# Half-block steps for two halves of the tokens, in the tail of a two-layer decoder kernel

## The reference, cut to what matters

```python
x = x + _L0_xattn_ref(_layernorm(x), ctx_2048, ...)   # softmax attention, 16 heads of 128
x = x + _L0_ffn_ref(_layernorm(x), ...)               # 8 experts of 176 units, top 2, plus 352 shared units
x = x + _L1_xattn_ref(_layernorm(x), ctx_2048, ...)   # linear attention, 16 heads of 16, relu features of 64
x = x + _L1_ffn_ref(_layernorm(x), ...)               # 8 experts of 176 units, top 2, normalised, plus 704 shared
```

```python
scores = jax.nn.softmax(x @ gate_w, axis=-1)
topk_w, topk_idx = jax.lax.top_k(scores, K)
comb = comb.at[jnp.arange(T)[:, None], topk_idx].add(topk_w)
g = silu(einsum('td,edh->teh', x, w_gate)) * einsum('td,edh->teh', x, w_up)
routed = einsum('teh,ehd,te->td', g, w_down, comb)
shared = silu(x @ sw_gate) * (x @ sw_up) @ sw_down
```

## Time and profile before

| | us |
|---|---|
| median of 3 runs | 1308.1 |
| lowest and highest | 1306.59 and 1308.49 |
| the profiled execution | 1307.69 |
| its span, first to last instruction | 1306.0 |
| around the span | 1.7 |

### The profile page before, as it was taken

How to read it: one execution, slowest core, us unless ns; L and a number is a source line. 1 busy time by engine, 2 the same in 40 slices (tenths; PEclk the granted TensorE clock), 3 DMA queues, 4 the chain that set the end, 5 groups by cost and what they waited for, 6 DMA issues and landing times. The chain is left out here.

```text
span 1306.0 us, 27038 instructions
## 1 busy us (share of the span) xinstructions
PE 1199.6 (92%) x9589; PEld 1044.7 (80%) x9589; DVE 884.8 (68%) x1829; ACT 732.5 (56%) x1285; POOL 538.6 (41%) x559
## 2 busy tenths in 40 slices
PE   5999999999879999999999999999999876997798
PEld 4888888889758888888788887888878776785586
DVE  5666656566657887878887788778886465555554
ACT  4656556556545666576665666666656433442443
POOL 2423232232225363553545535445364063562242
PEclk9999999999988999999999999999999967997799
DMA  4211111110031111011110111101000070022000
GB/s 144 69 42 56 39 34 53 39 39 1 2 90 53 48 48 48 1 47 47 47 47 0 47 47 34 60 0 47 0 1 1 1 246 20 2 115 86 1 1 15
DMA packets 38795, 56.04 MB, mean 43 GB/s; under 512 B 3106, under 2 KB 37202, under 8 KB 38226
## 3 DMA queue, kind: packets, MB, share of 16 engines
q1 hardware_dynamic: 37922, 54.23, 13.1%
q10 hardware_dynamic: 816, 1.05, 0.3%
HBM read 54.81 MB, written 0.46 MB: 42 GB/s over the span
## 5 line engine op out<-in xcount | busy, mean ns | idle before, releaser
L1118 POOL TENSOR_TENSOR att_sq<-att_work,att_sq 128x500 fp32r<-128x500 f32 x90 | 119.8, 1331 | 159.7 <-DVE att_sq L1018 159.7
L1122 POOL TENSOR_TENSOR attention_kk<-att_work,attention_kk 128x500 fp32r<-128x500 f32 x90 | 122.1, 1357 | 153.3 <-DVE attention_kk L1026 153.3
L102 PE MATMUL att_csum<-att_pT,att_cn 125*128 125x448 f32 x384 | 156.3, 407 | 5.1 <-DVE att_pT L1067 4.4
L944 ACT ACTIVATE att_pr<-att_pr,att_nmx 112x1500 f32<-112x1500 f32 (+1 forms) x96 | 108.5, 1130 | 72.4 <-DVE att_nmx L1055 72.4
L104 PE MATMUL att_csum<-att_pT,att_cn 125*128 125x448 f32 x384 | 141.1, 367 | 0.0
L103 PE MATMUL att_csum<-att_pT,att_cn 125*128 125x448 f32 x384 | 140.0, 365 | 0.0
L535 DVE SCALAR_TENSOR_TENSOR attention_kk<-kvs_keys_ps,kvs_bk,attention_kk 64x500 fp32r<-64x500 f32 x96 | 70.8, 738 | 91.7 <-ACT attention_kk L419 90.1
L1067 DVE TENSOR_TENSOR att_pT<-att_ring,att_pT 125x448 fp32r<-125x448 f32 x192 | 118.3, 617 | 21.7 <-ACT att_pT L960 21.5
L1052 DVE TENSOR_SCALAR_CACHE_REDUCE att_pr<-att_ring 112x500 f32<-112x500 f32 x192 | 121.8, 675 | 6.4 <-PE att_ring L104 5.0
L290 PE MATMUL kvs_feat<-kvs_f,attention_kk 128*125 128x256 f32 x768 | 113.0, 284 | 10.9 <-DVE kvs_kp L607 10.1
L877 PEld LDWEIGHTS att_ring<-all_ident,att_pr 112*125 112x125 f32 x768 | 110.9, 190 | 14.4 <-ACT att_pr L944 2.2
(11 more groups left out here) (279 smaller groups left out, 3276.9 us busy)
## 6 DMA issues: line engine op xcount, KB each, us to landing
attention_raw_t<-in_ctxT SPq DMA_DIRECT2D x45, 500.0 KB, 4.0
att_raw_n<-in_ctx SPq DMA_DIRECT2D x16, 750.0 KB
tail_gate_w<-in_gate SPq DMA_DIRECT2D x1, 2112.0 KB, 8.1
tail_up_w<-in_up SPq DMA_DIRECT2D x1, 2112.0 KB, 13.9
kvs_raw_q<-in_wq SPq DMA_DIRECT2D x8, 256.0 KB, 4.0
tail_wo_raw<-in_wo SPq DMA_DIRECT2D x4, 512.0 KB, 6.9
tail_down_w<-in_down SPq DMA_DIRECT2D x1, 2048.0 KB, 18.0
tail_gate_w<-in_gate SPq DMA_DIRECT2D x1, 1760.0 KB, 12.0
```

The costliest lines, as they stand in the source:

```text
L102: nc.tensor.matmul(out, w_lo, x_hi, start=start, stop=False, skip_group_check=True)
L944: nc.scalar.activation(pr[:, j, keys], pr[:, j, keys], ACT.Exp, scale=-1.0, bias=nmx[:, j:j + 1], accum_out=z[:, 4 * u + j, c:c + 1]).then ...
L1118: nc.gpsimd.tensor_tensor(sq[1][:, i % 2, :], work[:, i % 2, :], sq[0][:, i % 2, :].bitcast(F32), ALU.subtract).then_inc(sq_lo, 1)
L1122: nc.gpsimd.tensor_tensor(kk[:, c, 2 + gi, :], work[:, i % 2, :], kk[:, c, gi, :].bitcast(F32), ALU.subtract).then_inc(k_lo, 1)
```

## The change

`TT` = 4 tiles become two halves of 224 tokens (`H` = 2, `HT` = 224; tiles 0 and 1, tiles 2 and 3). The two mixtures are no longer two loops of 14 and 17 blocks over 448 tokens but one row of 62 half-blocks, `STEPS`: the 14 blocks of the first mixture for half 0, the same for half 1, the 17 blocks of the second for half 0, then for half 1. A loop over positions 0 to 64 runs on every engine. A step k is widened at position k (from step 28 on, k+1), spread at the same position save for a table of late ones, and narrowed two positions after its spread. Between these steps stand the other works of the other half: the norm and routing of half 1 during steps 0 to 12, the second norm, read-out and third norm of half 0 from position 15 to 28, during half 1's blocks of the first mixture, and those of half 1 from position 29 to 42, during half 0's blocks of the second mixture.

Core of the tables:

```diff
+STEPS = [(m, h, n) for m in range(2) for h in range(H) for n in range(BLOCKS[m])]
+WEIGHTED = (E * EU // 128, BLOCKS[1])
+FIRST1 = H * BLOCKS[0]
+SPLITS = [(0, n) for n in range(BLOCKS[0])] + [(1, n) for n in range(BLOCKS[0], BLOCKS[1])] + \
+         [(1, n) for n in range(BLOCKS[0])]
...
+FULLS, HIDS = 7, 4
...
+    return k if k < FIRST1 else k + 1
...
+def spread_at(k):
+    late = {0: 1, FIRST1: 33, FIRST1 + 1: 33, FIRST1 + 2: 34, FIRST1 + 3: 34, FIRST1 + 4: 35, FIRST1 + 5: 35,
+            FIRST1 + 6: 36, FIRST1 + 7: 36, FIRST1 + BLOCKS[1]: 47}
+    return late.get(k, widen_at(k))
```

```diff
+        dve.wait_ge(self.newton, 11 * h + 1)
+        nc.vector.tensor_scalar(self.rstd[:, y].bitcast(I32), self.var[:, y].bitcast(I32), -0.5, RSQRT_BITS,
+                                ALU.mult, ALU.add).then_inc(self.newton, 1)
...
+        dve.wait_ge(self.newton, n + 1)
+        nc.vector.scalar_tensor_tensor(self.tmp[:, y], self.tmp[:, y], -0.5, self.var[:, y], ALU.mult, ALU.mult)\
+            .then_inc(self.newton, 1)
+        dve.wait_ge(self.newton, n + 2)
+        nc.vector.scalar_tensor_tensor(self.rstd[:, y], self.tmp[:, y], 1.5, self.rstd[:, y], ALU.add, ALU.mult)\
```

On the tensor engine (the old order is removed whole; at r = 5 to 9 stand `features`, `read` and `turn` of the read-out):

```diff
+                    if t == 2 and i == 3:
+                        pe.wait_ge(wo.scaled, 2 * B)
+                        ln1.turn(pe, 0)
+                    if t == 3 and i == 1:
+                        router.logits(pe, 0, ln1)
+            for n in range(POSITIONS):
+                r, h = (n - 15) % 14, (n - 15) // 14
+                if n == 28:
+                    ln3.turn(pe, 0)
+                for k in steps_at(widen_at, n):
+                    moe.widen(pe, k)
+                if n == 1:
+                    router.turn(pe, 0)
+                for k in steps_at(spread_at, n):
+                    moe.spread(pe, k)
+                if n == 6:
+                    router.logits(pe, 1, ln1)
+                if n == 12:
+                    router.turn(pe, 1)
+                if h in (0, 1):
+                    if r == 4:
+                        lin.query(pe, h)
+                    if r == 5:
...
+                    if r == 10:
+                        lin.project(pe, h)
+                if n in (32, 46):
+                    router.turn(pe, 2 + (n - 32) // 14)
+                for k in range(len(STEPS)):
+                    if spread_at(k) + 2 == n:
+                        moe.narrow(pe, k)
+                if n == 4:
+                    ln1.turn(pe, 1)
+                if n in (18, 32):
+                    ln2.turn(pe, (n - 18) // 14)
+                if n == 42:
+                    ln3.turn(pe, 1)
+                if n in (28, 42):
+                    router.logits(pe, 2 + (n - 28) // 14, ln3)
```

On the scalar engine:

```diff
+            ln1.high(act, 0)
+            ln1.copy(act, 0)
+            moe.split_high(act, 3)
+            router.exponentials(act, 0)
+            act.wait_ge(wo.out_done, TT)
+            for n in range(POSITIONS):
...
+                for k in steps_at(widen_at, n):
+                    moe.silus(act, k)
...
+                for k in range(len(STEPS)):
+                    if spread_at(k) + 1 == n:
+                        moe.high(act, k)
+                if n in (12, 32, 46):
+                    router.high(act, {12: 1, 32: 2, 46: 3}[n])
+                if n < 10:
+                    moe.split_high(act, n + 4)
...
+                if n == 5:
+                    ln1.high(act, 1)
+                    ln1.copy(act, 1)
+                if n == 8:
+                    router.exponentials(act, 1)
...
+                if n in (28, 42):
+                    ln3.high(act, (n - 28) // 14)
+                    ln3.copy(act, (n - 28) // 14)
+                if n in (29, 43):
+                    router.exponentials(act, 2 + (n - 29) // 14)
+                if 20 <= n < 34:
+                    moe.split_high(act, n - 20 + 17)
```

On the vector engine, the first half's norm and routing stand ahead of the loop and all the rest in it; read-out and third norm are at the same positions as on PE (`h`, `r`):

```diff
+            wo.add(dve, 0, x_loaded)
+            ln1.statistics(dve, 0, wo.added, 1)
+            ln1.guess(dve, 0)
+            for i in range(3):
+                ln1.sharpen(dve, 0, i)
+            ln1.apply(dve, 0)
+            ln1.low(dve, 0)
+            router.start(dve, 0)
+            router.shares(dve, 0)
+            router.ranks(dve, 0)
+            router.weights(dve, 0)
+            for n in range(POSITIONS):
...
+                for k in steps_at(widen_at, n):
+                    moe.hidden(dve, k)
...
+                if n == 0:
+                    wo.add(dve, 1, x_loaded)
+                    ln1.statistics(dve, 1, wo.added, 2)
+                if n == 2:
+                    ln1.guess(dve, 1)
+                    ln1.sharpen(dve, 1, 0)
+                if n == 3:
+                    ln1.sharpen(dve, 1, 1)
+                    ln1.sharpen(dve, 1, 2)
+                    ln1.apply(dve, 1)
+                if n == 5:
+                    ln1.low(dve, 1)
+                if n == 7:
+                    router.start(dve, 1)
+                if n == 9:
...
+                    moe.add(dve, (n - 15) // 14)
+                if n in (16, 30):
+                    ln2.statistics(dve, (n - 16) // 14, moe.added, (n - 16) // 14 + 1)
+                    ln2.guess(dve, (n - 16) // 14)
+                    ln2.sharpen(dve, (n - 16) // 14, 0)
+                if n in (17, 31):
+                    ln2.sharpen(dve, (n - 17) // 14, 1)
+                    ln2.sharpen(dve, (n - 17) // 14, 2)
+                    ln2.apply(dve, (n - 17) // 14)
...
+                    if r == 11:
+                        ln3.statistics(dve, h, lin.added, h + 1)
+                        ln3.guess(dve, h)
+                        ln3.sharpen(dve, h, 0)
+                    if r == 12:
+                        ln3.sharpen(dve, h, 1)
+                        ln3.sharpen(dve, h, 2)
+                        ln3.apply(dve, h)
+                if n in (28, 42):
+                    ln3.low(dve, (n - 28) // 14)
+                if n in (29, 43):
+                    router.start(dve, 2 + (n - 29) // 14)
+                if n in (30, 44):
+                    router.shares(dve, 2 + (n - 30) // 14)
+                    router.ranks(dve, 2 + (n - 30) // 14)
+                if n in (31, 45):
+                    router.weights(dve, 2 + (n - 31) // 14)
+                if n in (48, POSITIONS - 1):
+                    moe.add(dve, 2 + (n > 48))
```

On POOL:

```diff
+            wo.low(pool, nc.gpsimd, 5)
+            moe.split_low(pool, 0)
+            wo.low(pool, nc.gpsimd, 7)
+            pool.wait_ge(wo.odd_lo, 4)
             pool.wait_ge(halves_set, 2)
-            moe0.set_member(pool, 0)
-            wo.low(pool, nc.gpsimd, 5)
-            pool.wait_ge(wo.odd_lo, 3)
-            moe0.set_member(pool, 1)
-            pool.wait_ge(moe0.member_done, 2)
...
-            moe1.set_member(pool, 0)
-            pool.wait_ge(moe1.member_done, 1)
-            moe1.set_member(pool, 1)
...
+            moe.set_member(pool, 0)
+            pool.wait_ge(moe.member_done, 1)
+            moe.set_member(pool, 1)
+            pool.wait_ge(moe.member_done, 2)
+            for i in range(1, len(SPLITS)):
+                moe.split_low(pool, i)
...
+                if i in (16, 28):
+                    lin.add_bias(pool, (i - 16) // 12)
```

1144 lines of the change are left out of this document (576 added, 568 removed).

## The result

The changed kernel takes 1321.59 us (median of 4 runs, 1320.04 to 1323.23) against 1307.34 us (4 runs, 1305.69 to 1308.49) of the kernel before in the same comparison. The ratio is 1.0108, with a 95% interval of 1.0095 to 1.0122: it is 1.1% slower. The profiled execution took 1321.45 us with a span of 1319.8; forecast were 1323.3 and 1321.6, and the range was 1303 to 1336. The total fits, so what is to be tested is whether its parts do, and why the overlap earned so little.

A forecast was written before the change was run, and what follows sets the result against it. PE bounds the mixtures' regular stretches and waits in the other stages. 1098.7 start + 154.9 half-steps + 24.5 small work + 38.5 waits + 5.0 behind the last matmul = 1321.6 span, + 1.7 = 1323.3 us; 8-in-10 range 1303 to 1336.

The forecast's parts named there:

- first half-block starts at: First mixture's start: first widening at 1098.7 us, not 1107.4; 1093 if no DVE operation meets POOL, 1103 if all small ones do.
- 62 half-steps: Both mixtures on PE: 56 weighted and 6 unweighted half-blocks take 154.9 us, whole ones 136.3; halving costs 18.6 us.
- steps 0 to 5: First mixture's start: PE waits for half 0's weights and half 1's norm turn, with slowed clock, together 10.2 us.
- steps 6 to 27: Rest of the first mixture, with half 0's read-out and second norm on half-loaded DVE and ACT: 2.5 us of waits.
- positions 28 to 33: Change of mixtures: third norm's turn, then DVE's 15 us row against 7 us of PE cover; waits and half clock 20.8 us.
- positions 40 to 47, and rest: Second mixture: 3 us of waits at half 1's third norm and routing, 2 us in the rest of the row.
- small PE work: Between half-blocks: norm turns, logits, weight turns, query, reads and projections keep their price, 24.5 us, within 22 to 31.
- the rival with cheap halves: Mixtures on PE: halves cost nothing, by the skill's formula, with the forecast's waits: 1311 us; chance 0.04.
- The wait of 4.6 us ahead of the turn of half 1: Position 4: PE waits 4.6 us as half 1's norm on DVE stands behind products, low halves and POOL collisions.
- the cover works: Whole tail: start at 1093, half 1's norm and routing in time, PE waits only 18.5 us: 1297.6 us; chance 0.16.
- POOL paces the splits: 14 steps at the start: POOL splits and DVE collisions exceed 2.5 us a position, PE waits 0.7 each: 1333 us; chance 0.12.
- the order serialises elsewhere: An unforeseen engine wait stops the row; overlap is lost in each half's read-out, 17 us idle returns: 1335 us; chance 0.06.

The follow-up runs named there:

- number 11: The kernel before, each whole block issued on PE as two half-blocks in turn (widen, spread, narrow): 1326.87 us against 1307.74, ratio 1.0137.
- number 2: The changed kernel with the first half of set_member ahead of batch 5's low half, the second behind the third split: 1320.8 us against 1307.56, ratio 1.0095.
- number 3: The changed kernel with matmuls that nobody reads put into four of PE's waits: 1322.59 us against 1307.56 of the kernel before, ratio 1.012.
- number 4: The changed kernel with the third routing on DVE ahead of most of half 1's second norm: 1317.35 us against 1307.56 of the kernel before, ratio 1.0075.
- number 7: The changed kernel with one Newton step per norm in place of three: 1315.2 us against 1308.42 of the kernel before, ratio 1.0049.
- number 10: The changed kernel without POOL's low halves of the second mixture's blocks 0 to 13, small memsets instead: 1317.75 us against 1307.74, ratio 1.007.
- number 6: The changed kernel with both routing exponentials computed by the silu function, so no table loads there: 1318.57 us against 1308.42, ratio 1.0064.
- number 5: The kernel before with matmuls that nobody reads in PE's waits at the norms and first spreads: 1302.89 us against 1308.42, ratio 0.995.
- number 9: The kernel before with nearly all PE waits filled, also ahead of the first projection and the logits: 1293.45 us against 1307.74, ratio 0.9909.
- number 12: The changed kernel with set_member early, third routing first, two Newton steps and PE's waits filled: 1310.88 us against 1308.87 of the kernel before, ratio 1.0016.
- number 8: The changed kernel with set_member early, third routing first and two Newton steps per norm: 1314.59 us against 1308.42 of the kernel before, ratio 1.0041.

## Why the prediction was right

**The sum by its terms.** Forecast and measured, in us:

| term | forecast | measured |
|---|---|---|
| first half-block starts at | 1098.7 | 1102.0 |
| 62 half-steps | 154.9 | 56 x 2.525 + 6 x 1.96 = 153.2 |
| waits and half clock, steps 0 to 5 | 10.2 | 3.3 + 5.1 = 8.4 |
| steps 6 to 27 | 2.5 | 1.7 |
| positions 28 to 33 | 20.8 | 5.4 + 1.8 + 8.9 + 6.8 = 22.9 |
| positions 40 to 47, and rest | 5.0 | 2.6 + 3.2 + 1.0 = 6.8 |
| small PE work | 24.5 | what is left: 19.9 |
| behind the last matmul | 5.0 | 4.9 |
| span | 1321.6 | 1319.8 |

The first summands of each wait are gaps, the last one is half the length of PE's work at clock 0.50 behind them (1107.6 to 1117.8, 1192.9 to 1203.1, 1216.7 to 1220.2, 1257.7 to 1264.6). The 19.9 of small PE work is the remainder and takes up the errors of the other terms. Added up in the trace from start to start of PE's matmuls behind 1102.0, the parts are half-steps 150.5, small work 22.9, gaps over 0.75 us 24.6 and, for half of the other time at clock 0.50, 14.9. The table's steps and its gaps both hold the matmul ahead of a gap, and some spreads stand side by side and are cheaper; that is where its remainder lost 3 us.

That the total came within 2 us is in part luck: the start was 3.3 us later than forecast, waits and half clock 1.0 more, the half-steps 4.4 less and the small work 1.6 less.

**The halving.** Right, and shown three times: 2.52 to 2.53 us a step in the changed kernel, the same in number 11, and 19.1 us for the whole against 18.6. The 0.112 us of the earlier trace rows hold in the mixtures: a widening of 224 columns starts every 0.111 us. The Trainium skill (TensorE: Matmul & The Clock Gate, Back-to-back issue gap) would have 96 ns by its formula for a single matmul, and the same section has about 81 ns at 128 and 131 ns at 512 columns for a stream with weight loads. The trace agrees with neither: 111 ns at 224 and 205 at 448 columns, so the rival with cheap halves had no ground.

**The start.** The mechanism was right and was priced too low: the two-column operations did end with POOL's, but four of them and both scalings did, so the turn of half 0 was 9.2 us late and the first widening 3.3 us later than forecast. How much of it is `set_member` stays open: in number 2, with one half of it moved away, 7.6 of the 9.4 us stay, as POOL's splits take that half's place and the other half meets the scalings. The Trainium skill (SBUF — State Buffer, SBUF: two separate sides) calls the port of DVE and GpSimd an exclusive lock, taken by a DVE operation in a two-port mode against any GpSimd one and by one with two inputs in SBUF against a GpSimd operation that reads SBUF. The trace agrees: the one-input L1193 is held 1.88 us by a memset and the two-input L1202 1.79 us by a select, while the two-input operations from 1089.38 on take 0.16 us beside a memset, whose row names no input. So moving POOL work helps only as far as what then stands beside the chain does not hold it.

**Steps 0 to 5.** The wait for the first spread was 3.3 us as forecast. The wait of 4.6 us ahead of the turn of half 1 did not come: PE ran at clock 0.50 from 1107.6 to 1117.8 and was itself late by as much. Number 3 shows the two to be one: with the clock kept up, the wait is 4.2 us and the turn stands at the same place. The prediction added 1.2 us of clock to each wait; it should have seen that a slow PE and a wait for DVE take the same time, not two times. Behind the turn this no longer holds: in number 3 half clock there cost 3.5 us.

**The change of mixtures.** Right in place and order, and nearly in size: 5.4 us ahead of `ln3.turn(0)` (5 forecast, with its clock in it), 1.8 and 8.9 ahead of the weight turn (2.6 and 8). The clock made 6.8 us; the prediction had it inside the first 5 and as 5 us at half clock behind the weights, which it took whole, though such a stretch costs half its length. Numbers 4, 7 and 10 each take a part away, DVE's order 4.9 us of the wait, Newton steps 1.2, POOL's splits 2.2. The table loads are in that chain, as predicted, but with about 1 us (number 6) and not with 2.6.

**Where the overlap's gain went.** Against number 11, which has the halves' price but no overlap, the changed kernel is only 5 us faster. PE's gaps over 0.75 us in the tail sum to 42.8 us, and to 44.8 before. The work that was to hide the norms and routings is there, but a half's routing on DVE is nearly as long as a whole one's: the first takes 4.1 us for two tiles (1099.3 to 1103.4) and took 4.5 for four. Its operations are small and their number sets the time. The same chain is run twice and its cover, four widenings and a narrow, is half as long. POOL's splits come on top where they stand beside such a chain, as at the third norm of half 0 and the second of half 1; the second norm of half 0 (from 1153.7) meets none and keeps its 0.16 us an operation. This paragraph is argued from the traces; no run changes the length of the cover alone.

**The rivals.** That the cover works fell: the start came at 1102 and not 1093. That POOL paces the splits fell: in 1127 to 1188 PE is busy 59.3 of 61 us beside POOL's splits. That the order serialises elsewhere fell too, behind the first widening every gap over 0.75 us is at a place that the prediction names or at most 1.7 us long. The 1335 of that last rival is not the sum of what it names: 1323.3 + 17 would be 1340.

**What stays open.** How the 15.4 us that the filled kernel gains divide between the clock and other effects of the fillers isn't settled; no run held the clock up without matmuls. The two groups of runs in numbers 5 and 9 speak for the clock: with the same fillers, runs at a lower clock were 10.5 and 8.8 us longer. Why the same program keeps its clock in one run and not in another isn't known, and no profile shows one of the longer runs. Nor is it shown what the changed kernel would take with all of `set_member` out of the norm's way.

## What to carry to other kernels

Before an overlap in halves, price a half step from rows with the short moving operand and count each change of stationary operand twice; set against it not the idle time of the bounding engine but the number of small operations in the chain that must fit behind the cover. Where one engine's idle time is followed by its own work on the path, first try to fill the wait with matmuls that nobody reads: that gave 0.9% here, where the reordering of the whole tail cost 1.1%. Read several runs and their clocks, not one: the fillers of number 5 worked in half of them. Then ask of each stretch which engine ends last there. From 1067 us on, 40 and 53 us less at half clock made the tail 9.6 and 15.4 us shorter in the old order (numbers 5 and 9), 28 and 27 us less made it 0.7 and 3.5 us shorter in the new one (numbers 3 and 12, the latter against number 8). And look at what follows a filled wait: a new wait that the fillers uncover can bring the half clock back at a worse place, as in number 3.

## What the runs showed of the hardware

- The clock: in the kernel before it stands at 0.50 behind PE's waits (1086.3 to 1093.2, 1100 to 1110.2, 1117 to 1120.5, 1175 to 1185.3 and three stretches more); with matmuls in the waits (number 9) there is none from 1067 to 1289 us. The 1.2 GHz stretches are worth 15.4 us there at the most.
- Around a spread (41 rows between matmuls of 128 rows) starts are further apart than the moving columns explain: (0.21 - 0.111) + (0.30 - 0.111) + (0.21 - 0.118) = 0.38 us with 224 columns, (0.29 - 0.205) + (0.40 - 0.205) + (0.21 - 0.118) = 0.37 with 448. It is a price of the change and not of the columns, and alternating half-blocks pay it twice: 5.04 - 4.69 = 0.35 us a block over side-by-side halves.
- A row of POOL splits of 0.72 us without a gap stretched neighbouring small DVE operations to 0.65 us each, four in a row (1207.8 to 1210.5); each ended within 0.03 us of a split's end.
- Small two-input DVE operations were held by a POOL select (1.79 us) and by splits (0.65 us), and not by a memset (0.16 us from 1089.38 on, beside one of 1.85 us); a one-input operation was held by a memset (1.88 us).
